# Cross attention of eight sequences: x in three buffers, first biases in step 4, h's high part behind the fourth head, and the mix's high part of the last step on VectorE

## The chip, the cores and the metric

The kernel runs on one core of a Trainium2 chip. The metric is the device time of one execution in microseconds (us). TensorE multiplies, VectorE, ScalarE and GpSimd (POOL) work element by element, SyncE (SP) issues most transfers.

## The reference

For eight sequences, x of 256 rows by 256 and a context of 256 rows by 192, with 16 heads of 64:

```python
h = _layernorm(x, gamma, beta)
Q = (h @ Wq).reshape(B, NQ, N_HEADS, HEAD_DIM)
K = (context @ Wk).reshape(B, NC, N_HEADS, HEAD_DIM)
V = (context @ Wv).reshape(B, NC, N_HEADS, HEAD_DIM)
attn = jnp.einsum('bihd,bjhd->bhij', Q, K)
attn = jax.nn.softmax(attn, axis=-1) * scale
vals = jnp.einsum('bhij,bjhd->bihd', attn, V).reshape(B, NQ, INNER)
out = vals @ Wo + bo
return x + out
```

## The kernel before

Every large product is made to near fp32 precision from two fp32r parts: an operand is rounded to its high part (ScalarE mostly), the remainder is its low part (VectorE or GpSimd), and TensorE sums high x high, high x low and low x high in PSUM.

The work is cut into 32 steps, four to a sequence; a step handles two pairs of heads, that is four heads. A program for each engine walks the steps -1 to 33 in the same order, and semaphores tie them together. In step u TensorE makes the scores of u (`scores`), mixes V with the probabilities of step u - 1 (`mix`), projects keys and queries of u + 1 (`keys`, `queries`), adds step u - 1's share of the output to `o_ps` (`output`), makes a tile of V two steps ahead or so (`values`) and turns the scaled probabilities of u (`turn`, L989). ScalarE takes the exponentials (L475), the high part of the mix (L502) and of keys and queries (L485), and copies half of the turned probabilities. VectorE takes the maxima (L674), the inverses of the sums (L681), the low part of the mix (L739) and of keys and queries (L699), scales the fourth head (L689) and copies the other half of the turned probabilities (L779). GpSimd scales the first three heads (L383).

Between these stand the jobs of a sequence, placed by `of_seq(u, offset)`: x and its context are loaded five steps before the sequence's first (`LOAD`), VectorE's statistics of x stand in that step too (`STATS`, L600), GpSimd's reciprocal deviation (L328) and norm (L336) one step later with TensorE's turn of the context, TensorE's turn of the normed x one more (`TURN_X`), h split into high part (VectorE, L760) and low part (GpSimd, L365) two steps ahead (`SPLIT_H`: steps 2, 6, ..., 26), and then GpSimd adds the output's bias to x (L352), which VectorE adds to the finished sum (L724) for the store. Sequences 0 and 1 have places of their own: statistics of 1 at the end of step 0, deviation and norm of 1 first in GpSimd's step 1, bias 0 at the end of GpSimd's step 2 and bias 1 at the end of step 4.

x has two buffers. SyncE's load of x of sequence 2 overwrites that of sequence 0, so it waits in step 3 for sequence 0's norm and bias (L286). The 25 pieces of the weights are loaded at the start and split during steps -1 to 4: the high parts on ScalarE (L423), the low parts on VectorE (L593) for the pieces in `LO_VECTOR` and on GpSimd (L322) for those in `LO_POOL`. Pieces 8, 9 and 20, 21 are Wv. For V, GpSimd copies the context's parts from `c_t` to `c_val` (L347).

PSUM has three pairs of banks in a ring, a bank for the mix and one for the output. In the last step with output through `output` (u = 31) the keys, queries and values of later steps are missing, so little stands between the mix and the output (L957); `last_output` (L973) ends the last sequence.

Of the kernel before, what the change touches and what calls it, by code (L numbers as in the profile page):

```python
# [6 lines left out]
def cross_attention_block(nc, x, ctx_in, w_q, w_k, w_v, w_o, b_o, gamma, beta, out):  # L7
# [10 lines left out]
    P = 128  # L18
# [15 lines left out]
    LOOP_STEPS, LOOPS = 2 * PER_SEQ, 3  # L34
# [27 lines left out]
    LO_VECTOR = (0, 4, 5, 8, 9, 13, 20, 21)  # L62
    LO_POOL = (1, 2, 3, 6, 7, 10, 11, 12, 14, 15, 16, 17, 18, 19, 22, 23)
    WARM = 6
    SHIFT = 16
    V_HALF = GROUP * P // 2

    with ExitStack() as ctx:
# [37 lines left out]
        x_in = sb("x_in", [P, 2, RT, D])  # L106
# [37 lines left out]
        x_banks = ring[2]  # L144
# [15 lines left out]
        x_loaded = [sem("x_loaded0"), sem("x_loaded1")]  # L160
# [53 lines left out]
        def walk(engine, step, first):  # L214

            for u in range(-1, first):
                step(u, lambda n: 0)
            with engine.Fori(0, LOOPS) as turn:  # L220
                for u in range(first, first + LOOP_STEPS):
                    step(u, lambda n: turn * n)
            for u in range(first + LOOP_STEPS * LOOPS, LAST):
                step(u, lambda n: 0)

# [16 lines left out]
        def _(sp):  # L242
            def number(n):
                return n if isinstance(n, int) else sp.snap(n)

# [20 lines left out]
            def load_x(b, sequence):  # L266
                sp.dma_start(x_in[:, b % 2, :, :], x_v[sequence]).then_inc(x_loaded[b % 2], 16)

            def load_c(b, sequence):
                sp.dma_start(c_in[:, b % 2, :, :], c_v[sequence]).then_inc(c_loaded[b % 2], 16)  # L270

            load_x(0, 0)
            for n in range(0, 10):
                load_weight(n)
            load_x(1, 1)
            load_c(1, 1)
# [3 lines left out]
            def step(u, turns):  # L280
                b = of_seq(u, LOAD, 2)
                if b is not None:
                    sequence, used = number(b + turns(2)), number(b - 1 + turns(2))

                    sp.wait_ge(x_norm_ready, used)
                    sp.wait_ge(x_bias_ready, used)  # L286
                    load_x(b, sequence)
                    sp.wait_ge(c_turned, used)
                    load_c(b, sequence)
                b = of_seq(u, PUT)  # L290
                if u == LAST - 1:

                    sp.wait_ge(y_ready, SEQS)
                    sp.dma_start(y_v[SEQS - 1, :, 0, :], y_sb[:, b % 2, 0, :])\
                        .then_inc(y_free[b % 2], 16)
                elif b is not None:
                    sequence, added = number(b + turns(2)), number(b + 1 + turns(2))
                    sp.wait_ge(y_ready, added)
                    sp.dma_start(y_v[sequence], y_sb[:, b % 2, :, :]).then_inc(y_free[b % 2], 16)

            walk(sp, step, 3)
# [5 lines left out]
        def _(pool):  # L307
# [23 lines left out]
            def norm(b):  # L331
# [3 lines left out]
                for r in range(RT):  # L335
                    last = nc.gpsimd.tensor_scalar(x_norm[:, r, :], x_in[:, b % 2, r, :],  # L336
# [4 lines left out]
            def context_for_values(b):  # L341

                if b >= 2:
# [6 lines left out]
            def bias(b):  # L350
                for r in range(RT):
                    last = nc.gpsimd.tensor_tensor(x_bias[:, b % 2, r, :], x_in[:, b % 2, r, :],  # L352
# [6 lines left out]
            pool.dma_start(bo_b[:, :], b_o.partition_broadcast(P)).then_inc(bo_in, 16)  # L359
            context_for_values(0)  # L360
# [8 lines left out]
            def step(u, turns):  # L369
# [3 lines left out]
                if b is not None:  # L373
                    deviation(b)
                    norm(b)
# [21 lines left out]
                b = of_seq(u, SPLIT_H, 1)  # L397
                if u == 2:
                    weight_lo(22)

                    pool.wait_ge(bo_in, 16)
                    bias(0)

                b = 1 if u == PER_SEQ else b if u > PER_SEQ else None
                if b is not None:
                    if b >= 2:

                        pool.wait_ge(y_ready, b - 1)

                    pool.wait_ge(x_norm_ready, b + 1)  # L410
                    bias(b)

            for u in range(-1, LAST):
                step(u, lambda n: 0)

        @block.scalar
        def _(act):
# [42 lines left out]
            def step(u):  # L460
# [39 lines left out]
                elif 1 <= u < STEPS:  # L500
# [85 lines left out]
        def _(dve):  # L586
# [10 lines left out]
            def rows_statistics(b, r):  # L597
                k = b % 2
                dve.wait_ge(x_loaded[k], 16 * (b // 2 + 1))
# [20 lines left out]
            def norm(b):  # L620
                dve.wait_ge(rstd_ready, b + 1)
                for r in range(RT):
                    last = nc.vector.tensor_scalar(x_norm[:, r, :], x_in[:, b % 2, r, :],
                                                   mean_var[:, r, 0:1], rstd[:, r:r + 1],
                                                   ALU.subtract, ALU.mult)
                last.then_inc(x_norm_ready, 1)
# [27 lines left out]
            def step(u):  # L654
# [73 lines left out]
                if u == 0:  # L728
                    weight_lo(8)
                    weight_lo(9)  # L730
                if u == STEPS:
# [5 lines left out]
                elif 1 <= u < STEPS:  # L737
# [16 lines left out]
                if u < 2:  # L754
                    last_head()
# [17 lines left out]
                if 0 <= u < STEPS:  # L773
# [8 lines left out]
                    if u == 0:  # L782
                        statistics(1)
# [330 lines left out]
```

## Time and profile before

| | us |
|---|---|
| median of 3 runs | 339.98 |
| lowest, highest run | 339.65, 396.95 |
| the profiled execution's own time | 339.38 |
| its span, first to last instruction | 337.3 |

The page counts the busy time of each engine inside the span; the time outside it, 2.1 us, is start and end of the program. Matmuls overlap, so TensorE's busy share says that it was supplied, not that it ran at its peak. "PEclk" is the granted clock in tenths of the full speed. In a list of instructions, a number in brackets is the idle time of the engine before the instruction, and what ended it.

### The profile page before, as it was taken

Reading aid. Unit: us, or ns where it says so; the run is one execution under the profiler, and the core shown is the slowest. Engines: PE = TensorE matmul, PEld = TensorE weight load, DVE = VectorE, ACT = ScalarE, POOL = GpSimd, SP = SyncE. Lnnn points to the kernel's source line nnn. Section 1 sums busy time; section 2 is a strip of 40 time slices with the busy share of each in tenths; the row PEclk is TensorE's granted clock in tenths of the full one; section 3 lists DMA queues with packets and bytes.
Section 4 is the critical chain, followed back from the end, with each engine's and each line's share of the span. In section 5 each row is a group of like instructions: output and inputs, shape, how many; then the busy total and the mean of one; then the engine's idle time right before and its main releaser. Section 6 shows DMA issues by size and latency. Waiting matters only on the chain.

```text
span 337.3 us, 9748 instructions
## 1 busy us (share of the span) xinstructions
PE 322.7 (96%) x3773; PEld 283.2 (84%) x3773; DVE 258.4 (77%) x585; ACT 254.7 (76%) x799; POOL 161.3 (48%) x294
## 2 busy tenths in 40 slices
PE   5999997999999999999999999999999999999986
PEld 4868777888889988888998888899888889988864
DVE  4898855787887788787877878877887878668764
ACT  4898883888778877787677887778777876777872
POOL 4688954463563364631563435633646315333330
PEclk9999997999999999999999999999999999999999
DMA  6860001020000200002000200002000010001000
GB/s 182 258 186 2 1 26 32 2 82 7 2 3 2 87 0 3 2 2 87 1 3 2 81 10 2 0 3 88 2 2 0 2 34 2 2 0 34 2 3 31
DMA packets 10764, 10.70 MB, mean 32 GB/s; under 512 B 960, under 2 KB 10176, under 8 KB 10720
## 3 DMA queue, kind: packets, MB, share of 16 engines
q1 hardware_dynamic: 10192, 9.64, 9.3%
q8 instruction: 30, 0.49, 0.6%
q10 hardware_dynamic: 416, 0.33, 0.3%
q0 software_dynamic: 112, 0.13, 0.2%
q14 instruction: 14, 0.11, 0.1%
HBM read 8.00 MB, written 2.10 MB: 30 GB/s over the span
## 4 chain that ended last, share of the span: by engine, by line
PE 78%; ACT 9%; DVE 6%; POOL 4%; issue 1%; DMA 1%; DVEq 0%; SPq 0%; POOLq 0%; ACTq 0%
PE mix_ps L866 15%; PE ring_ps L837 12%; PE ring_ps L932 11%; PE o_ps L957 10%; PE ring_ps L890 9%; PE ring_ps L989 8%; PE ring_ps L1023 6%; ACT prob L475 4%; DVE prob L689 2%; PE ring_ps L1030 2%; ACT qk_hi L485 2%; PE ring_ps L910 1%; PE o_ps L798 1%; POOL prob L383 1%; POOL wo_lo L322 1%
## 5 line engine op out<-in xcount | busy, mean ns | idle before, releaser
L383 POOL TENSOR_SCALAR prob<-prob,inv 128x256 f32<-128x256 f32 x192 | 90.3, 488 | 121.7 <-DVE inv L681 121.7
L475 ACT ACTIVATE prob<-ring_ps,neg_max 128x256 f32<-128x256 f32 x256 | 118.3, 474 | 21.7 <-DVE neg_max L674 21.7
L674 DVE TENSOR_REDUCE neg_max<-ring_ps 128x2 f32<-128x512 f32 x128 | 81.3, 677 | 1.0 <-PE ring_ps L837 0.8
L866 PE MATMUL mix_ps<-prob_t,v_sb 128*64 128x256 f32 x504 | 61.5, 385 | 0.5 <-DVE prob_t L779 0.5
L779 DVE COPY prob_t<-ring_ps 128x512 f32<-128x512 f32 x64 | 41.9, 687 | 21.6 <-PE ring_ps L989 20.3
L699 DVE TENSOR_TENSOR qk_lo<-ring_ps,qk_hi 128x512 fp32r<-128x512 f32 x64 | 44.1, 689 | 15.6 <-ACT qk_hi L485 15.6
L475 ACT ACTIVATION_READ_ACCUMULATOR prob<-ring_ps,neg_max 128x1 f32 x256 | 52.8, 206 | 0.0
L485 ACT ACTIVATE qk_hi<-ring_ps 128x512 fp32r<-128x512 f32 x64 | 38.7, 605 | 14.1 <-PE ring_ps L932 14.1
L866 PEld LDWEIGHTS mix_ps<-prob_t,v_sb 128*64 128x64 f32 x504 | 33.4, 136 | 18.3 <-issue 0.6
L989 PE MATMUL ring_ps<-ident,prob 64*128 64x64 f32 x1024 | 38.6, 223 | 1.8 <-DVE prob L689 1.1
L837 PE MATMUL ring_ps<-qk_hi 64*128 64x256 f32 x256 | 39.9, 301 | 0.3 <-DVE qk_lo L699 0.3
L957 PE MATMUL o_ps<-wo_hi,mix_hi 128*128 128x256 f32 x124 | 35.2, 284 | 4.3 <-DVE mix_lo L739 4.0
L989 PEld LDWEIGHTS ring_ps<-ident,prob 64*128 64x128 f32 x1024 | 36.2, 138 | 3.3 <-issue 1.7
L546 ACT ACTIVATE v_sb<-ring_ps 128x256 f32<-128x256 f32 x58 | 19.1, 381 | 25.9 <-PE ring_ps L1030 25.9
L560 ACT ACTIVATE prob_t<-ring_ps 128x512 f32<-128x512 f32 x64 | 35.8, 605 | 3.5 <-PE ring_ps L989 3.5
L837 PE MATMUL ring_ps<-qk_hi,qk_lo 64*128 64x256 f32 x256 | 36.8, 277 | 0.0
L837 PE MATMUL ring_ps<-qk_lo,qk_hi 64*128 64x256 f32 x256 | 36.8, 277 | 0.0
L890 PEld LDWEIGHTS ring_ps<-c_t,w_hi 128*128 128x128 f32 x192 | 26.5, 188 | 11.7 <-issue 11.5
L890 PE MATMUL ring_ps<-c_t,w_hi 128*128 128x256 f32 x192 | 35.5, 294 | 0.0
L957 PE MATMUL o_ps<-wo_lo,mix_hi 128*128 128x256 f32 x124 | 34.9, 281 | 0.0
L957 PE MATMUL o_ps<-wo_hi,mix_lo 128*128 128x256 f32 x124 | 34.8, 281 | 0.0
L681 DVE RECIPROCAL inv<-sums 128x2 f32<-128x2 f32 x128 | 20.9, 163 | 16.7 <-ACT prob L475 11.1
(116 smaller groups left out, 697.0 us busy)
## 6 DMA issues: line engine op xcount, KB each, us to landing
x_in<-in_x_dram SPq DMA_DIRECT2D x8, 256.0 KB, 2.9
out_dram<-y_sb SPq DMA_DIRECT2D x7, 256.0 KB, 2.2
c_in<-in_ctx_dram SPq DMA_DIRECT2D x7, 192.0 KB, 2.8
w_raw<-in_L_xattn_Wq_dram SPq DMA_DIRECT2D x8, 128.0 KB, 3.4
w_raw<-in_L_xattn_Wo_dram SPq DMA_DIRECT2D x4, 256.0 KB, 6.3
w_raw<-in_L_xattn_Wk_dram SPq DMA_DIRECT2D x4, 128.0 KB, 3.8
w_raw<-in_L_xattn_Wk_dram SPq DMA_DIRECT2D x8, 64.0 KB, 3.5
w_raw<-in_L_xattn_Wv_dram SPq DMA_DIRECT2D x2, 256.0 KB, 5.1
```

Of the source, the lines that this page charges most:

```text
L383: last = nc.gpsimd.tensor_scalar(prob[:, e, r, :], prob[:, e, r, :], inv[:, e, r:r + 1], SCALE, ALU.mult, ALU.mult)
L475: last = nc.scalar.activation(prob[:, e, r, :], score_bank(u, e)[:, r * ROWS:(r + 1) * ROWS], ACT.Exp, bias=neg_max[:, e, r:r + 1], accum_ ...
L485: nc.scalar.activation(qk_hi[:, a, :, 0:ROWS], qk_banks(u + 1)[a][:, :].rearrange("p (a b) -> p a b", b=ROWS), ACT.Copy)\
L674: nc.vector.tensor_reduce(neg_max[:, e, :], score_bank(u, e)[:, :].rearrange("p (r j) -> p r j", r=RT), AX, ALU.max, negate=True).then_inc ...
L699: nc.vector.tensor_tensor(qk_lo[:, a, :, 0:ROWS], qk_banks(u + 1)[a][:, :] .rearrange("p (a b) -> p a b", b=ROWS), qk_hi[:, a, :, 0:ROWS]. ...
L779: nc.vector.tensor_copy(turned_half(e), score_bank(u, e)[:, :] .rearrange("p (k i) -> p k i", i=HALF))\
L837: last = nc.tensor.matmul(score_bank(u, 2 * a + h)[:, r * ROWS:(r + 1) * ROWS], q[own, a, 1, r * P:(r + 1) * P], key[own, a, 0, 0:ROWS], s ...
L866: last = nc.tensor.matmul(ps[h * HALF:(h + 1) * HALF, first:first + ROWS], v_sb[:, w // RT % 2, j, p * P + h * HALF:p * P + (h + 1) * HALF ...
L890: nc.tensor.matmul(ps[:, 0:ROWS], w[:, i, cols], c_t[:, b % 2, k, :], start=not shared and w is w_hi and i == K0 and k == 0, stop=w is pas ...
L932: last = nc.tensor.matmul(ps[:, ROWS:2 * ROWS], w[:, Q0 + d, cols], h[:, b % 2, d, :], start=n == 0 and d == 0, stop=n == 2 and d == DT - ...
L957: last = nc.tensor.matmul(o_ps[:, r * D:(r + 1) * D], m[:, a, r * P:(r + 1) * P], wt[:, o, cols], start=s == 0 and a == 0 and n == 0 and r ...
L989: last = nc.tensor.transpose(score_bank(u, 2 * a + half)[:, k * HALF:(k + 1) * HALF], prob[own, 2 * a + h, r, j * P:(j + 1) * P], ident[ow ...
```

## The change

- x has three buffers, each with its semaphore. SyncE's loads of x wait for the norm and the bias of three sequences before; that of sequence 2 waits for nothing. The load of the bias vector `bo` moves from GpSimd's queue to SyncE's, behind the weights. SyncE's loop is written out.
- GpSimd's biases 0 and 1 both stand at the end of step 4.
- In steps from 2 on, VectorE makes h's high part behind the fourth head (behind both low parts of the keys and `deviation_base`). In step 2 its pieces 20 and 21 come ahead, right behind the first low part of the keys; `variance` of a measured sequence stands where it stood.
- Piece 8 is split on GpSimd before step 0 in place of VectorE in step 0. The values of sequence 0 read `c_t`; its copy to `c_val` is gone.
- The statistics of x 1 are spread over VectorE's step 0, and its norm goes from GpSimd to VectorE's step 1, one half on each side of the first low part of the keys.
- Around step 0 the ring's pairs of banks are named so that step 1's second pair of scores waits for the first pair's turned probabilities only.
- In step 31 VectorE makes the mix's high part (a copy) as well as its low part, with the third inverse between them; TensorE does the eight products of the high part first, then the four of the low part. The last output has its high products first too.

```diff
-    LO_VECTOR = (0, 4, 5, 8, 9, 13, 20, 21)
-    LO_POOL = (1, 2, 3, 6, 7, 10, 11, 12, 14, 15, 16, 17, 18, 19, 22, 23)
+    LO_VECTOR = (0, 4, 5, 9, 13, 20, 21)
+    LO_POOL = (1, 2, 3, 6, 7, 8, 10, 11, 12, 14, 15, 16, 17, 18, 19, 22, 23)
+    X_BUFS = 3
-        x_in = sb("x_in", [P, 2, RT, D])
+        x_in = sb("x_in", [P, X_BUFS, RT, D])
         def qk_banks(u):
-            return ring[u % 3]
+            return ring[u % 3 if u else 2]
         def score_bank(u, e):
-            return ring[(u - (e // 2 if u else 1 - e // 2)) % 3][e % 2]
+            return ring[(u - e // 2) % 3][e % 2]
-        x_banks = ring[2]
+        x_banks = ring[0]
...
             for n in range(10, len(PIECES)):
                 load_weight(n)
+            sp.dma_start(bo_b[:, :], b_o.partition_broadcast(P)).then_inc(bo_in, 16)
-            def step(u, turns):
+            def step(u):
                 b = of_seq(u, LOAD, 2)
                 if b is not None:
-                    sp.wait_ge(x_norm_ready, used)
-                    sp.wait_ge(x_bias_ready, used)
-                    load_x(b, sequence)
-                    sp.wait_ge(c_turned, used)
-                    load_c(b, sequence)
+                    if b >= X_BUFS:
+                        sp.wait_ge(x_norm_ready, b - X_BUFS + 1)
+                        sp.wait_ge(x_bias_ready, b - X_BUFS + 1)
+                    load_x(b)
+                    sp.wait_ge(c_turned, b - 1)
+                    load_c(b)
...
             def context_for_values(b):
-                if b >= 2:
+                if b >= 3:
                     pool.wait_ge(v_made, PER_SEQ * (b - 1))
...
             for n in (1, 2, 3, 6, 7):
                 weight_lo(n)
-            pool.dma_start(bo_b[:, :], b_o.partition_broadcast(P)).then_inc(bo_in, 16)
-            context_for_values(0)
+            weight_lo(8)
...
                 if b is not None:
                     deviation(b)
-                    norm(b)
+                    if b >= 2:
+                        norm(b)
...
                 if u == 2:
                     weight_lo(22)
-                    pool.wait_ge(bo_in, 16)
-                    bias(0)
-                b = 1 if u == PER_SEQ else b if u > PER_SEQ else None
-                if b is not None:
-                    if b >= 2:
-                        pool.wait_ge(y_ready, b - 1)
-                    pool.wait_ge(x_norm_ready, b + 1)
-                    bias(b)
+                for b in (0, 1) if u == PER_SEQ else (of_seq(u, SPLIT_H, 2),):
+                    if b is not None:
+                        if b == 0:
+                            pool.wait_ge(bo_in, 16)
+                        if b >= 2:
+                            pool.wait_ge(y_ready, b - 1)
+                        pool.wait_ge(x_norm_ready, b + 1)
+                        bias(b)
...
         @block.scalar
-                elif 1 <= u < STEPS:
+                elif 1 <= u < STEPS - 1:
                     act.wait_ge(mixed, u)
...
         @block.vector
                 if u == 0:
-                    weight_lo(8)
                     weight_lo(9)
+                    rows_statistics(1, 0)
...
-                elif 1 <= u < STEPS:
+                elif u == STEPS - 1:
+                    dve.wait_ge(mixed, u)
+                    nc.vector.tensor_copy(mix_hi[:, :, :].rearrange("p a b -> p (a b)"),
+                                          mix_ps[:, :]).then_inc(mix_hi_ready, 1)
+                    inverse(2)
+                if 1 <= u < STEPS:
                     dve.wait_ge(mix_hi_ready, u)
...
-                inverse(2)
+                if u != STEPS - 1:
+                    inverse(2)
...
+                if u == 1:
+                    dve.wait_ge(x_turned, 1)
+                    norm(1, (0,))
                 keys_lo(0)
+                if u == 0:
+                    rows_statistics(1, 1)
+                if u == 1:
+                    norm(1, (1,))
+                if u == 2:
+                    weight_lo(20)
+                    weight_lo(21)
                 if measured is not None:
                     variance(measured)
                 if u == -1:
                     weight_lo(5)
                 if u < 2:
                     last_head()
+                keys_lo(1)
+                if u == 0:
+                    variance(1)
+                if measured is not None:
+                    deviation_base(measured)
+                if u >= 2:
+                    last_head()
                 b = of_seq(u, SPLIT_H, 1)
                 if b is not None:
                     for d in range(DT):
                         dve.wait_ge(h_full_ready, DT * b + d)
                         nc.vector.tensor_copy(h_hi[:, b % 2, d, :], h_full[:, d, :])\
                             .then_inc(h_hi_ready, 1)
-                if u == 2:
-                    weight_lo(20)
-                    weight_lo(21)
-                keys_lo(1)
-                if measured is not None:
-                    deviation_base(measured)
-                if u >= 2:
-                    last_head()
...
                     if u == 0:
-                        statistics(1)
+                        deviation_base(1)
                         weight_lo(13)
...
             def scores(u):
-                            pe.wait_ge(prob_t_ready[h], BATCH * (u - 1) + (2 if u == 1 else 1))
+                            pe.wait_ge(prob_t_ready[h], BATCH * (u - 1) + 1)
...
             def output(w):
+                if w == STEPS - 2:
+                    pe.wait_ge(mix_hi_ready, w + 1)
+                    for m, weights in ((mix_hi, (wo_hi, wo_lo)), (mix_lo, (wo_hi,))):
+                        if m is mix_lo:
+                            pe.wait_ge(mix_lo_ready, w + 1)
...
             def last_output():
                 for a in range(BATCH):
-                    pe.wait_ge(mix_lo_ready, STEPS + a)
+                    pe.wait_ge(mix_hi_ready, STEPS + a)
                     for r in range(RT):
...
+                    pe.wait_ge(mix_lo_ready, STEPS + a)
+                    for r in range(RT):
...
             def values(n):
-                pe.wait_ge(c_val_ready, b + 1)
+                tiles = c_val if b else c_t
+                if b:
+                    pe.wait_ge(c_val_ready, b)
```

## Rows read from the trace of the kernel before

**Rows 1.** The page: busy time by engine with share; granted clock by slice.
```profile
PE 322.7 (96%) x3773; PEld 283.2 (84%) x3773; DVE 258.4 (77%) x585; ACT 254.7 (76%) x799; POOL 161.3 (48%) x294
PEclk9999997999999999999999999999999999999999
```

**Rows 2.** TensorE's waits over the span: us in total, times, longest.
```profile
PE o_ps L957 <- DVE mix_lo L739: 4.0, 2, 2.6
PE ring_ps L989 <- DVE prob L689: 1.1, 6, 0.2
```

**Rows 3.** Stretches: length; busy PE, PEld, DVE, ACT, POOL; granted clock; DMA.
```profile
12.56:20.72 8.16, 7.50 (x82) 6.11 (x84) 7.63 (x17) 8.08 (x27) 7.38 (x14) 1.00 0.83 263
...
43.76:57.72 13.96, 11.40 (x124) 10.15 (x120) 7.50 (x22) 7.99 (x26) 8.58 (x12) 0.88 0.12 34
...
77.68:87.56 9.88, 9.70 (x124) 8.51 (x120) 8.38 (x18) 7.46 (x24) 5.70 (x10) 1.00 0.00 1
87.56:97.09 9.53, 9.53 (x123) 8.45 (x121) 7.63 (x22) 6.82 (x24) 4.46 (x8) 1.00 0.01 2
```

**Rows 4.** Timeline of step 3: start, duration, then idle time and releaser last.
```profile
47.05 1.44 POOL L352 TENSOR_TENSOR x_bias<-x_in,bo_b 128x256 f32<-128x256 f32 x2
...
48.72 0.39 SPq L267 DMA_DIRECT2D x_in<-in_x_dram  x1
...
51.44 0.43 DVE L600 BATCH_NORM_STATS2 bn<-x_in 128x6 f32<-128x256 f32 x1 [3.67 <-DMA x_in<-in_x_dram]
...
52.60 0.55 PE L957 MATMUL o_ps<-wo_hi,mix_hi 128*128 128x256 f32 x1 [2.56 <-DVE mix_lo L739]
```

**Rows 5.** One stretch behind that wait, same columns.
```profile
53.00:54.00 1.00, 1.00 (x6) 1.00 (x6) 1.00 (x5) 0.00 (x0) 0.56 (x2) 0.50 0.00 0
```

**Rows 6.** Timeline of GpSimd: its first heads in step 9.
```profile
110.26 1.85 POOL L383 TENSOR_SCALAR prob<-prob,inv 128x256 f32<-128x256 f32 x4 [2.30 <-DVE inv L681]
```

**Rows 7.** Timeline of steps 6 and 7: h, fourth head, turned probabilities.
```profile
84.02 0.49 DVE L760 CAST h_hi<-h_full 128x256 fp32r<-128x256 f32 x2
84.59 1.44 POOL L365 TENSOR_TENSOR h_lo<-h_full,h_hi 128x256 fp32r<-128x256 f32 x2 [0.47 <-DVE h_hi L760]
85.58 1.33 DVE L689 TENSOR_SCALAR prob<-prob,inv 128x256 f32<-128x256 f32 x2
...
95.49 0.62 DVE L689 TENSOR_SCALAR prob<-prob,inv 128x256 f32<-128x256 f32 x2
96.92 1.29 DVE L779 COPY prob_t<-ring_ps 128x512 f32<-128x512 f32 x2 [0.81 <-PE ring_ps L989]
```

**Rows 8.** Timelines of GpSimd, TensorE and VectorE, steps -1 to 2.
```profile
13.71 0.60 POOL L359 DMA_DIRECT2D bo_b<-in_L_xattn_bo_dram  x1
14.32 1.08 POOL L347 CAST c_val<-c_t 128x256 fp32r<-128x256 f32 x3
...
17.88 0.73 PE L1011 MATMUL mix_ps<-wv_lo,c_val 128*128 128x512 f32 x2 [0.36 <-DVE wv_lo L593]
...
25.26 2.44 POOL L336 TENSOR_SCALAR x_norm<-x_in,mean_var,rstd 128x256 f32<-128x256 f32 x2 [0.19 <-POOL rstd L328]
...
30.55 0.71 PE L989 MATMUL ring_ps<-ident,prob 64*128 64x64 f32 x16 [0.27 <-POOL prob L383]
...
39.12 1.82 DVE L593 TENSOR_TENSOR wv_lo<-w_raw,wv_hi 128x512 fp32r<-128x512 f32 x2
...
41.00 0.74 PE L1011 MATMUL mix_ps<-wv_lo,c_val 128*128 128x512 f32 x2 [0.49 <-DVE wv_lo L593]
```

**Rows 9.** Timeline of the last steps: the mix's parts, the output, the last sums.
```profile
326.03 0.60 ACT L502 ACTIVATE mix_hi<-mix_ps 128x512 fp32r<-128x512 f32 x1
...
326.66 0.69 DVE L739 TENSOR_TENSOR mix_lo<-mix_ps,mix_hi 128x512 fp32r<-128x512 f32 x1 [0.33 <-ACT mix_hi L502]
...
327.41 0.38 PE L957 MATMUL o_ps<-wo_hi,mix_hi 128*128 128x256 f32 x1 [1.42 <-DVE mix_lo L739]
...
334.28 0.76 DVE L668 TENSOR_TENSOR y_sb<-ring_ps,y_sb 128x256 f32<-128x256 f32 x2 [0.78 <-PE ring_ps L973]
```

More of the change, by code:

```diff
@@ L33, in cross_attention_block @@
     STEPS = SEQS * PER_SEQ
-    LOOP_STEPS, LOOPS = 2 * PER_SEQ, 3
     LAST = STEPS + 2
@@ L159, in cross_attention_block @@
         w_in = [sem(f"w_in{i}") for i in range(len(PIECES))]
-        x_loaded = [sem("x_loaded0"), sem("x_loaded1")]
+        x_loaded = [sem(f"x_loaded{k}") for k in range(X_BUFS)]
         c_loaded = [sem("c_loaded0"), sem("c_loaded1")]
@@ L212, in of_seq @@
             return b if rest == 0 and first <= b < SEQS else None
[L214 to L224, printed above, removed]
         def before(n, pieces):
@@ L296, in step @@
                 elif b is not None:
[L297 to L301, printed above, removed]
+                    sp.wait_ge(y_ready, b + 1)
+                    sp.dma_start(y_v[b], y_sb[:, b % 2, :, :]).then_inc(y_free[b % 2], 16)
+            for u in range(-1, LAST):
+                step(u)
             sp.wait_ge(y_free[0], 16 * (SEQS // 2 + 1))
@@ L367, in hidden_lo, with step @@
                                             ALU.subtract).then_inc(h_lo_ready, 1)
-            def step(u, turns):
+            def step(u):
                 if u == 1:
@@ L618, in statistics, with norm @@
                 deviation_base(b)
-            def norm(b):
+            def norm(b, rows=range(RT)):
                 dve.wait_ge(rstd_ready, b + 1)
-                for r in range(RT):
-                    last = nc.vector.tensor_scalar(x_norm[:, r, :], x_in[:, b % 2, r, :],
+                for r in rows:
+                    last = nc.vector.tensor_scalar(x_norm[:, r, :], x_in[:, b, r, :],
                                                    mean_var[:, r, 0:1], rstd[:, r:r + 1],
                                                    ALU.subtract, ALU.mult)
-                last.then_inc(x_norm_ready, 1)
+                if r == RT - 1:
+                    last.then_inc(x_norm_ready, 1)
             def context_lo(b, ps):
@@ L949, in output @@
                     pe.wait_ge(y_ready, b)
+                if w == STEPS - 2:
[3 more added lines that the diff above has]
+                            pe.wait_ge(mix_lo_ready, w + 1)
+                        for a in range(BATCH):
+                            o, cols = divmod(BATCH * s + a, GROUP)
+                            cols = slice(cols * D, (cols + 1) * D)
+                            for r in range(RT):
+                                for wt in weights:
+                                    last = nc.tensor.matmul(
+                                        o_ps[:, r * D:(r + 1) * D], m[:, a, r * P:(r + 1) * P],
+                                        wt[:, o, cols], start=False, stop=False,
+                                        skip_group_check=True)
+                    last.then_inc(o_added, 1)
+                    return
                 pe.wait_ge(mix_lo_ready, w + 1)
@@ L966, in last_output @@
                 for a in range(BATCH):
[L967 removed]
                     o, cols = divmod(PAIRS - BATCH + a, GROUP)
                     cols = slice(cols * D, (cols + 1) * D)
+                    pe.wait_ge(mix_hi_ready, STEPS + a)
                     for r in range(RT):
[L971 to L976 removed]
+                        for n, wt in enumerate((wo_hi, wo_lo)):
+                            nc.tensor.matmul((ring[2][1], ring[1][0])[r][:, 0:D],
+                                             mix_hi[:, a, r * P:(r + 1) * P], wt[:, o, cols],
+                                             start=a == 0 and n == 0, stop=False,
+                                             skip_group_check=True)
+                    pe.wait_ge(mix_lo_ready, STEPS + a)
+                    for r in range(RT):
+                        last = nc.tensor.matmul((ring[2][1], ring[1][0])[r][:, 0:D],
+                                                mix_lo[:, a, r * P:(r + 1) * P], wo_hi[:, o, cols],
+                                                start=False, stop=a == BATCH - 1,
+                                                skip_group_check=True)
                         if a == BATCH - 1:
@@ L1010, in values @@
                             low_ready(pe, FOR_V[g])
-                        last = nc.tensor.matmul((mix_ps, o_ps, mix_ps)[n][:, :], c_val[:, b % 2, k, rows],
+                        last = nc.tensor.matmul((mix_ps, o_ps, mix_ps)[n][:, :], tiles[:, b % 2, k, rows],
                                                 w[:, i, first:first + PIECE],
@@ L1022, in values @@
                             low_ready(pe, FOR_V[g])
-                        nc.tensor.matmul(ps[:, 0:V_HALF], c_val[:, b % 2, k, rows],
+                        nc.tensor.matmul(ps[:, 0:V_HALF], tiles[:, b % 2, k, rows],
                                          w[:, i, first + a * V_HALF:first + (a + 1) * V_HALF],
@@ L1026, in values @@
                 pe.wait_ge(c_rest_ready, b + 1)
-                high = (c_rest[:, b % 2, rows], c_val[HALF:P, b % 2, 1, rows])
+                high = (c_rest[:, b % 2, rows], tiles[HALF:P, b % 2, 1, rows])
                 for a, ps in enumerate(qk_banks(n)):
```

34 lines of the change are left out of this document (12 added, 22 removed).

## The prediction

> **What bounds the kernel now.** I read the page's engine table and its forty slices first. TensorE is busy 96% of 337.3 us, no other engine over 77%, and the granted clock stands at its full level except in one slice [rows 1]. So only stretches in which TensorE waits or runs at the low clock can give time back; work saved elsewhere counts only if it ends such a stretch. The list of TensorE's waits names two kinds that this change touches: the output products waiting for the mix's low part, 4.0 us in two places, and the transposes of probabilities waiting for the fourth head, six times [rows 2].
>
> Next I cut the span at the starts of the scores of one step to those of the next. Step 7, from 87.56 us, has nothing special: 9.53 us with TensorE never idle. Step 3, from 43.76, does the same TensorE work in 13.96 us; step 6, from 77.68, again the same work, takes 9.88 us, with 0.18 us of idle in it [rows 3]. Those excesses, 4.43 us and 0.35 us, are the two large terms below. Steps 0 to 2 and the last step I read in the timeline.
>
> **Step 3: x in three buffers, first bias later.** The chain is: GpSimd adds the first bias at 47.05 us for 1.44 us; only then may SyncE issue x of sequence 2, at 48.72; VectorE sits 3.67 us until it lands and starts its statistics at 51.44; the low part of the mix stands behind them, and TensorE starts the output at 52.60 after 2.56 us of idle [rows 4]. The idle is followed by a granted clock of 0.50, which is 1.2 GHz [rows 5]; that is why the step lost more than its idle. With a third buffer x of sequence 2 has a place of its own, and SyncE issues it right behind the weights with no wait at all. c of sequence 2 behind it waits only for the turn of c 0, long done; the result of sequence 0 is next in that queue and is not wanted before step 5. When this stall goes, what is late next in step 3? The same queue of VectorE as in step 7, where its statistics stand in the same place and TensorE never waits. The low part of Wo for that step is made on GpSimd ahead of where the bias was, so it isn't moved back; the heads on GpSimd come 1.44 us earlier. So step 3 becomes a step 7: minus 4.43 us (bounds 2.56, if the low clock stays for another reason, and 4.43).
>
> What this costs elsewhere: biases 0 and 1 both stand at the end of GpSimd's step 4, 2 x 1.44 = 2.88 us instead of 1.44. In the step that answers to it four steps on (no bias there) GpSimd idles 2.30 us before its first heads [rows 6]; so they start 2.88 - 2.30 = 0.6 us late. These heads are in place long before TensorE turns them at the end of a step of 10 us. Zero; with that cover gone it would be 0.6 us once. The load of the bias vector moves from GpSimd's queue to the end of SyncE's, where only step 4 needs it. Later x loads wait for an older bias than before: zero.
>
> **The high part of h behind the fourth head (steps 2, 6, ..., 26).** Now VectorE makes h's high part at 84.02 (0.49 us for two), GpSimd at once makes the low part at 84.59 (1.44 us) and then a bias, and the fourth head's two scalings, which begin at 85.58, take 1.33 us; one step on, with GpSimd idle, the same two take 0.62 us [rows 7]. The 0.71 us reach TensorE as the 0.18 us of idle before the second half of its turn, and with what stands behind that, as 0.35 us of the step [rows 3]. With h behind the fourth head GpSimd waits until the scalings are over. The two h copies, 0.49 us, then fall in the 0.81 us that VectorE waits before its copy of turned probabilities [rows 7], so nothing is pushed. GpSimd's low part moves about 2.5 us, to the end of the step; the queries that use it are in the next step, after scores and mix. Six such steps stand between 77 us and 284 us (the six waits of [rows 2]): 6 x 0.35 = 2.1 us, and the step 2 case is counted with the start. Bounds 0 (the collision just takes another form) and 2.1 us, since a step like step 7 has no idle left to give.
>
> The Trainium skill, SBUF — State Buffer, section "Who interferes with whom", says that GpSimd and a VectorE scaling or cast in its two-port mode exclude each other for a whole instruction, and that a copy out of PSUM isn't among these. The trace agrees in size, 1.33 us against 0.62 us. By the rule the moved h copies, with GpSimd idle, cost their 0.49 us; if they met GpSimd's work they would double to about 1 us, which is past the cover of 0.81 us.
>
> **The start, steps 0 to 2.** Step 0: VectorE drops one of two splits of Wv, so TensorE's low Wv products, which start at 17.88, can start 0.5 us earlier; GpSimd takes that split (128x512, two inputs: as much as the two 128x256 of h, 1.44 us [rows 7]) and loses the bias DMA, 0.60, and the first copy of c, 1.08 us [rows 8]: even. VectorE's statistics of x 1, two of 0.43 us [rows 4] and small ones, go between other work of step 0; they push the fourth head and the low part of the keys a little, so of the 0.5 us about 0.25 are left at the step's end. Reading c_t in place of the copy changes no size. The bank names swapped around step 0 remove a wait that TensorE, busy turning c, doesn't feel now.
> Step 1: GpSimd's norm of x 1 takes 2.44 us, and its heads behind it hold TensorE's turn of the probabilities, its second half to 30.55 [rows 8]. On VectorE the same norm is two scalings, 0.62 us free and 1.33 us against GpSimd [rows 7]. That frees GpSimd and puts VectorE's fourth head in its place as the last: 0.4 to 0.9 us gained, I take 0.65 with the 0.25 of step 0 included, as VectorE is now the tight one.
> Step 2: VectorE's two splits of Wv at 39.12 take 1.82 us beside GpSimd's work, and TensorE waits 0.49 us for the second [rows 8]. Moved ahead of the two h copies (0.49 us [rows 7]) they end at least that much earlier, so the wait goes: 0.5 us, bounds 0 and 0.9 us. Together the start gives 1.15 us, bounds 0.2 and 2.
>
> **The last two steps.** Now ScalarE makes the high part at 326.03 (0.60 us), VectorE the low part at 326.66 (0.69), and TensorE, idle 1.42 us, starts at 327.41 [rows 9]. VectorE can't begin the high part before two inverses, at about 326.25; a copy of 512 from PSUM to SBUF costs it about 0.65 us (its copies of turned probabilities, 1.29 us for two [rows 7]), so TensorE starts its eight high products at about 327.0 and finds the low part made at about 327.8, ready when they are through: 0.4 us. ScalarE is 0.5 us ahead with the third and fourth head's probabilities, so the turn behind isn't late. I take 0.45 us. The last output with high products first: its last sums run on VectorE one after the other, 0.76 us for both [rows 9], and the first can't start much earlier; 0.1 us. Together 0.55 us, bounds 0 and 1.
>
> **Sum.** 4.43 + 2.1 + 1.15 + 0.55 = 8.2 us. The profiled execution itself took 339.38 us, 2.1 us more than its span and 0.6 us less than the shown median of 339.98: 339.4 - 8.2 = 331.2 us. No engine takes a new load on the path, and as TensorE has no idle in a step like step 7, nothing gained early is given back later.
>
> **Rivals.**
> Start or end don't pay. ScalarE is busy 8.08 of step 0's 8.16 us [rows 3]; if it or VectorE's new norm ends last, the 1.15 + 0.55 us shrink to about 0.2: 332.7 us. Against it: in step 1 it is GpSimd that TensorE waits for.
> The h move only shifts the collision, to the copy behind or the next step's heads: 2.1 us stay, 333.3 us. For it: GpSimd still has the same work beside VectorE; against it: the 0.81 us of cover.
> Step 3 gives only its idle: another wait of half a microsecond there, or a low clock all the same, leaves 1.9 us: 333.1 us.
> TensorE bound and the change without effect: if the 96% were true work, nothing moves, 339.4 us. Against it: 13.96 us against 9.53 for the same instructions.
> Slower: the third x buffer shifts every tensor behind it in SBUF by 2 KB a partition, the probabilities that TensorE turns among them. A step has 32 such pairs of transposes in about 1 us; were they slower by over a quarter (8.2 us over 32 steps is 0.26 us a step), the gain would be gone, and at double time it would be 339.4 - 8.2 + 32 = 363 us. No row shows a dependence on place, so this is the least likely.
>
> **How the numbers follow.** Forecast 0.60; start and end without pay 0.14; h 0.09; step 3 in part 0.08; without effect 0.06; slower 0.03. The likeliest gives 331.2. Low: start and end at their upper bounds give 0.85 + 0.45 = 1.3 us more, 329.9; for places where TensorE waits less than these rows show I go 0.9 us further, to 329.0. High: the cases at 333.3, with 333.6. A time faster by 2% is under 333.2 us (about what a measurement of this kernel can tell from no change). The forecast, the start case, and some half of the two cases at that edge lie below it, less a little for two small losses together: 0.76; within 2%: 0.21; slower: 0.03.
>
> **What would show it.** Right: step 3 at about 9.5 us with no low clock after the start; x of sequence 2 landed by about 25 us; steps 6, 10, ... at 9.5 us with the fourth head's scalings at 0.62 us for two; no wait on GpSimd's heads in step 1; the last output's wait near 1.0 us. Wrong: a wait of VectorE for x, copies of turned probabilities that start later than 0.81 us behind the fourth head, transposes that take longer everywhere, or a new low-clock stretch.

## The result and the profile after

| us | before | after |
|---|---|---|
| median | 339.81 (4 runs) | 331.37 (4 runs, 331.17 to 331.65) |
| profiled execution | 339.38 | 331.32 |
| its span | 337.3 | 329.3 |

One of the four runs before took 396.95 us, a slow run, and the ratio leaves it out; the other three lie between 339.49 and 339.98. The ratio is 0.9755, with a 95% interval of 0.9736 to 0.9774. On another chip the kernel after took 331.21 us (5 runs, 331.04 to 331.4), ratio 0.9764 [0.9741, 0.9788]. The forecast was 331.2.

The page of the kernel after, engine table and granted clock, to be laid beside [rows 1]:

```profile
PE 319.2 (97%) x3773; PEld 281.7 (86%) x3773; DVE 253.8 (77%) x587; ACT 253.2 (77%) x798; POOL 155.5 (47%) x289
PEclk9999999999999999999999999999999999999999
```

The slice at the low clock is gone. TensorE's waits in the kernel after:

```profile
PE ring_ps L1015 <- DVE prob L676: 1.0, 1, 1.0
PE o_ps L965 <- DVE mix_hi L727: 1.0, 1, 1.0
PE mix_ps L870 <- DVE prob_t L783: 0.5, 1, 0.5
```

The six waits of 0.2 us for the fourth head and the one of 2.6 us [rows 2] are gone. One wait for the fourth head, of 1.0 us, is new; it stands in step 1 and was not foreseen. The stretches from one step's scores to the next, with the columns of [rows 3]; they are steps 0, 1, 2, 3 and 6, 7:

```profile
12.50:20.13 7.63, 7.30 (x83) 6.20 (x84) 7.31 (x20) 7.56 (x26) 5.82 (x10) 1.00 0.96 272
20.13:31.83 11.70, 10.48 (x121) 8.59 (x118) 10.62 (x25) 10.23 (x32) 8.23 (x13) 1.00 0.32 98
31.83:43.14 11.31, 11.03 (x123) 9.56 (x123) 7.98 (x19) 9.78 (x31) 6.70 (x11) 1.00 0.01 1
43.14:52.72 9.58, 9.58 (x123) 8.51 (x120) 7.90 (x22) 7.98 (x26) 6.87 (x13) 1.00 0.00 0
72.68:82.19 9.51, 9.51 (x124) 8.43 (x120) 7.34 (x18) 7.07 (x24) 3.27 (x7) 1.00 0.01 3
82.19:91.70 9.51, 9.51 (x124) 8.43 (x120) 7.82 (x22) 7.08 (x24) 6.75 (x12) 1.00 0.01 2
```

Steps 3, 6 and 7 are now alike, 9.58, 9.51 and 9.51 us. From the starts of the scores in the two timelines (steps 1, 2, 3, 4 and 31: 20.72, 31.77, 43.76, 57.72 and 322.45 us before; 20.13, 31.83, 43.14, 52.73 and 315.03 after) and the two spans, each term can be read by itself:

| place | gain, measured in the two traces | forecast |
|---|---|---|
| up to the end of step 1 | -0.06 us (up to the end of step 0: +0.59; step 1: -0.65) | 0.65 |
| step 2 | 0.68 | 0.5 |
| step 3 | 4.37 | 4.43 |
| steps 4 to 30, six of them with h | 2.43 | 2.1 |
| from step 31 on | 0.58 | 0.55 |
| sum | 8.0 | 8.2 |

### The profile page after: what moved, and what is told of

Its sections match the earlier page's. It is cut to its first block, busy times and chain, and to the rows that moved or that the text cites. A ratio compares the mean times of both kernels' runs of the same rounds, so it can differ in the third digit from the quotient of the medians.

```text
span 329.3 us, 9691 instructions
## 1 busy us (share of the span) xinstructions
PE 319.2 (97%) x3773; PEld 281.7 (86%) x3773; DVE 253.8 (77%) x587; ACT 253.2 (77%) x798; POOL 155.5 (47%) x289
## 4 chain that ended last, share of the span: by engine, by line
PE 88%; ACT 5%; DVE 3%; POOL 2%; issue 1%; DVEq 0%; POOLq 0%; ACTq 0%
PE mix_ps L870 16%; PE ring_ps L841 13%; PE o_ps L978 12%; PE ring_ps L936 12%; PE ring_ps L894 10%; PE ring_ps L1015 9%; PE ring_ps L1052 8%; PE ring_ps L1059 3%; ACT prob L461 3%; PE ring_ps L914 1%; PE o_ps L802 1%; PE mix_ps L815 1%; PE mix_ps L807 1%; DVE prob_t L783 1%; DVE qk_lo L686 1%
## 5 line engine op out<-in xcount | busy, mean ns | idle before, releaser
L370 POOL TENSOR_SCALAR prob<-prob,inv 128x256 f32<-128x256 f32 x192 | 89.0, 480 | 106.1 <-DVE inv L668 105.9
L783 DVE COPY prob_t<-ring_ps 128x512 f32<-128x512 f32 x64 | 41.2, 686 | 21.0 <-PE ring_ps L1015 21.0
L1015 PE MATMUL ring_ps<-ident,prob 64*128 64x64 f32 x1024 | 37.5, 223 | 1.0 <-DVE prob L676 1.0
L978 PE MATMUL o_ps<-wo_hi,mix_hi 128*128 128x256 f32 x120 | 33.3, 278 | 0.5 <-POOL wo_lo L309 0.3
L978 PE MATMUL o_ps<-wo_lo,mix_hi 128*128 128x256 f32 x120 | 33.3, 277 | 0.0
L978 PE MATMUL o_ps<-wo_hi,mix_lo 128*128 128x256 f32 x120 | 33.2, 276 | 0.0
```

What stands on the lines that cost most here:

```text
L370: last = nc.gpsimd.tensor_scalar(prob[:, e, r, :], prob[:, e, r, :], inv[:, e, r:r + 1], SCALE, ALU.mult, ALU.mult)
L783: nc.vector.tensor_copy(turned_half(e), score_bank(u, e)[:, :] .rearrange("p (k i) -> p k i", i=HALF))\
L978: last = nc.tensor.matmul(o_ps[:, r * D:(r + 1) * D], m[:, a, r * P:(r + 1) * P], wt[:, o, cols], start=s == 0 and a == 0 and n == 0 and r ...
L1015: last = nc.tensor.transpose(score_bank(u, 2 * a + half)[:, k * HALF:(k + 1) * HALF], prob[own, 2 * a + h, r, j * P:(j + 1) * P], ident[ow ...
```

## The experiments

**The third buffer alone.** On the kernel before: x in three buffers, SyncE's load of x 2 free, bias 0 moved.

```diff
-                    sp.wait_ge(x_norm_ready, used)
-                    sp.wait_ge(x_bias_ready, used)
+                    if b >= 3:
+                        sp.wait_ge(x_norm_ready, b - 2)
+                        sp.wait_ge(x_bias_ready, b - 2)
...
                     weight_lo(22)
+                if u == PER_SEQ:
                     pool.wait_ge(bo_in, 16)
+                    pool.wait_ge(x_norm_ready, 2)
                     bias(0)
```

> The kernel before with only the third buffer for x, SyncE's load of x 2 without a wait, and bias 0 moved to the end of step 4. Theory A (the load of x 2 behind the first bias is the whole excess of step 3, idle and low clock): step 3 falls from 13.96 to about 9.55 us and the time by 4.4, to 335.5 us. Rival B (the idle goes but the low clock or another wait of the step stays): a fall of 2.6 us, to 337.3 us. Rival C (the gains of the other parts hang on this one or the other way round): less than 2 us or more than 6.

335.22 us, ratio 0.9881 [0.9854, 0.9907] to the kernel before on that chip (339.36), which is 4.1 us. Its step 3 runs from 43.49 to 53.24 us, 9.75. Theory A holds; half of the whole gain is this one load. The profiled execution was the slowest of the four (335.94 us), and its steps 3, 7, 8 and 27 to 30 each took 0.13 to 0.18 us longer than in the traces of the kernels before or after, at full clock. What slows them is not known.

**The wait, not the buffer.** The kernel after, in which SyncE's load of x 2 waits all the same: for bias 0, put back to the end of step 2, and in a second kernel only for GpSimd's low part of piece 22, which ends earlier.

```diff
                 if b is not None:
+                    if b == 2:
+                        sp.wait_ge(x_bias_ready, 1)
...
                     weight_lo(22)
-
-                for b in (0, 1) if u == PER_SEQ else (of_seq(u, SPLIT_H, 2),):
+                    pool.wait_ge(bo_in, 16)
+                    bias(0)
+
+                for b in (1,) if u == PER_SEQ else (of_seq(u, SPLIT_H, 2),):
```

> The kernel after, with bias 0 back at the end of step 2 and SyncE's load of x 2 waiting for it although its buffer is free. Theory A (the wait, not the buffer, is the cost): TensorE idles about 2.6 us in step 3, the clock then falls to half, the step takes about 14 us, 335.8 us in all. Rival B (the low clock before had another cause, such as the order of the start): idle of 2.6 us but full clock, 334.0 us.

```diff
                 if b is not None:
+                    if b == 2:
+                        sp.wait_ge(w_lo_pool_ready, before(23, LO_POOL))
```

> The kernel after, with SyncE's load of x 2 waiting for GpSimd's low part of piece 22, 1.4 us before where bias 0 would end. Theory A (part of the price is the clock that falls behind a long wait): TensorE idles about 1.3 to 1.6 us; if the clock holds, the time is 332.8 us, if it falls as it did behind 2.6 us, 334.5 us. This run tells whether the half wait already pays the clock.

One execution each: 335.82 us with the full wait, 332.88 with the half. TensorE's wait in the first, then the granted clock (third value from the end) behind it:

```profile
51.75 0.36 PE L982 MATMUL o_ps<-wo_hi,mix_hi 128*128 128x256 f32 x1 [2.35 <-DVE mix_lo L736]
...
53.00:54.00 1.00, 1.00 (x7) 1.00 (x6) 0.96 (x5) 0.00 (x0) 0.51 (x1) 0.50 0.00 0
```

And in the second:

```profile
50.49 0.36 PE L980 MATMUL o_ps<-wo_hi,mix_hi 128*128 128x256 f32 x1 [1.08 <-DVE mix_lo L734]
...
51.00:52.00 1.00, 1.00 (x11) 1.00 (x10) 1.00 (x6) 0.00 (x0) 0.44 (x1) 1.00 0.00 0
```

Behind 2.35 us of idle the clock stood at 0.50, its lower level of 1.2 GHz; behind 1.08 us it stayed full. The step took 13.77 us (43.18 to 56.95) with the full wait and 11.02 (43.18 to 54.20) with the half. With its free buffer in place the kernel pays the old price as soon as the load waits again, which is theory A; one execution of each kernel says so. The half wait also costs more than its idle: the first output product stands 7.31 us into the step in place of 6.05 in the kernel after (49.19 - 43.14), 1.26 us later where the trace counts 1.08.

**h's high part, undone.** The kernel after with the two copies back ahead of the keys' second low part.

```diff
+                b = of_seq(u, SPLIT_H, 1)
+                if b is not None:
+                    for d in range(DT):
+                        dve.wait_ge(h_full_ready, DT * b + d)
+                        nc.vector.tensor_copy(h_hi[:, b % 2, d, :], h_full[:, d, :])\
+                            .then_inc(h_hi_ready, 1)
                 keys_lo(1)
...
                 if u >= 2:
                     last_head()
-                b = of_seq(u, SPLIT_H, 1)
-                if b is not None:
...
```

> The kernel after with one part undone: VectorE makes h's high part again ahead of the second low part of the keys, in steps 2, 6, ..., 26. Theory A: each of the six steps from 6 to 26 goes back to about 9.9 us, the time rises by 2.1 to 2.4, to 333.6 us, and the fourth head's two scalings take 1.33 us there. Rival B (the move brought nothing, the gain came from the smaller queue of GpSimd): 331.4 us.

333.77 us, ratio 0.9838 [0.9811, 0.9864]. Step 6 in its timelines of VectorE, GpSimd and TensorE:

```profile
79.38 1.44 POOL L351 TENSOR_TENSOR h_lo<-h_full,h_hi 128x256 fp32r<-128x256 f32 x2 [0.48 <-DVE h_hi L765]
80.37 1.33 DVE L676 TENSOR_SCALAR prob<-prob,inv 128x256 f32<-128x256 f32 x2
...
81.86 0.71 PE L1015 MATMUL ring_ps<-ident,prob 64*128 64x64 f32 x16 [0.18 <-DVE prob L676]
```

The pattern of [rows 7] is back, 1.33 us and 0.18 us of idle, and with it 2.4 to 2.5 us: theory A.

**Is it VectorE's order or GpSimd's neighbour?** The same kernel as h_back, but GpSimd holds h's low part, and so the bias behind it, until the fourth head is scaled.

```diff
                 pool.wait_ge(h_hi_ready, DT * b)
+                pool.wait_ge(scaled_vector, PER_SEQ * b + SPLIT_H + 1)
```

> The same as h_back, VectorE's order as before, but GpSimd holds h's low part until the fourth head is scaled. Theory A (the cost is GpSimd's two-input subtraction running beside VectorE's scalings, not VectorE's order): the scalings take 0.62 us, the steps 9.5 us, 331.4 us as the kernel after. Rival B (the cost is that h's two copies stand ahead of the keys' second low part and the fourth head): 333.6 us as h_back.

331.31 us (331.28 to 331.32), on the same chip as the 333.77. In its step 6:

```profile
78.81 0.48 DVE L766 CAST h_hi<-h_full 128x256 fp32r<-128x256 f32 x2
79.25 0.69 DVE L687 TENSOR_TENSOR qk_lo<-ring_ps,qk_hi 128x512 fp32r<-128x512 f32 x1
80.17 0.17 DVE L669 RECIPROCAL inv<-sums 128x2 f32<-128x2 f32 x1 [0.22 <-ACT prob L462]
80.36 0.62 DVE L677 TENSOR_SCALAR prob<-prob,inv 128x256 f32<-128x256 f32 x2
```

VectorE's order is that of the kernel before, its scalings take 0.62 us, and all of the gain is there: theory A again. So the move of h was worth its 2.4 us only because it kept GpSimd's work, the subtraction and the start of the bias behind it, off VectorE's scalings; a wait on GpSimd does the same.

**The norm of x 1 back on GpSimd.**

```diff
                     deviation(b)
-                    if b >= 2:
-                        norm(b)
+                    norm(b)
...
-                if u == 1:
-                    dve.wait_ge(x_turned, 1)
-                    norm(1, (0,))
                 keys_lo(0)
-                if u == 1:
-                    norm(1, (1,))
```

> The kernel after with the norm of x 1 back on GpSimd in step 1. Theory A (the move paid nothing: TensorE's turn began at 30.60 us with it and at 30.55 before): 331.4 us, within 0.4, with TensorE now waiting for GpSimd's heads. Rival B (the prediction's term for step 1, hidden by something else in the kernel after): 332.0 us.

330.96 us (330.68 to 330.98), 0.35 less than the 331.31 of h_back_hold on the same chip, whose step 1 is that of the kernel after (11.73 us against 11.70). GpSimd and TensorE in step 1:

```profile
27.45 2.80 POOL L369 TENSOR_SCALAR prob<-prob,inv 128x256 f32<-128x256 f32 x6
...
30.30 0.71 PE L1008 MATMUL ring_ps<-ident,prob 64*128 64x64 f32 x16 [0.26 <-POOL prob L369]
```

Within the 0.4 us of theory A, but on the side of a small loss: moved as it was, the norm cost 0.35 us. That is not all of step 1's loss. Steps 0 and 1 of this kernel, laid beside the 8.16 and 11.05 us of the kernel before:

```profile
12.52:20.12 7.60, 7.30 (x82) 6.16 (x82) 7.27 (x20) 7.53 (x26) 5.79 (x10) 1.00 0.86 254
20.12:31.53 11.41, 10.56 (x122) 8.57 (x118) 9.71 (x23) 10.21 (x32) 10.49 (x15) 1.00 0.35 105
```

With GpSimd's norm where it was, step 1 still takes 0.36 us more than before.

**GpSimd's subtractions of step 1 behind the fourth head.** The kernel after, one wait more:

```diff
+                if u == 1:
+                    pool.wait_ge(scaled_vector, 2)
                 for n in {0: (10, 11, 12), 1: (15, 16, 17, 18)}.get(u, ()):
                     weight_lo(n)
```

> The kernel after, with GpSimd in step 1 holding the low parts of the weights' pieces 15 to 18 until the fourth head is scaled. Theory A (the norm's move was worth its price, but the freed GpSimd started these subtractions at 28.78 us, on the fourth head's scalings, 1.39 us in place of 0.62): the scalings take 0.62 us, TensorE's turn begins its second half at about 29.9 in place of 30.60, the time falls by 0.7, to 330.7 us. Rival B (ScalarE's or GpSimd's later work sets the end of step 2 anyway): 331.4 us.

330.13 us, ratio 0.9728 [0.9705, 0.9751]. Step 1 in the kernel after, VectorE, GpSimd and TensorE:

```profile
28.54 0.42 DVE L609 TENSOR_SCALAR x_norm<-x_in,mean_var,rstd 128x256 f32<-128x256 f32 x1
28.78 1.52 POOL L309 TENSOR_TENSOR w_lo<-w_raw,w_hi 128x256 fp32r<-128x256 f32 x2
29.06 1.39 DVE L676 TENSOR_SCALAR prob<-prob,inv 128x256 f32<-128x256 f32 x2
30.60 0.71 PE L1015 MATMUL ring_ps<-ident,prob 64*128 64x64 f32 x16 [1.01 <-DVE prob L676]
```

and in this one:

```profile
28.83 0.61 DVE L678 TENSOR_SCALAR prob<-prob,inv 128x256 f32<-128x256 f32 x2
29.53 1.42 POOL L309 TENSOR_TENSOR w_lo<-w_raw,w_hi 128x256 fp32r<-128x256 f32 x2 [0.95 <-DVE prob L678]
...
29.59 0.71 PE L1017 MATMUL ring_ps<-ident,prob 64*128 64x64 f32 x16 [0.24 <-DVE prob L678]
```

The scalings fall from 1.39 to 0.61 us and TensorE's wait from 1.01 to 0.24, which is theory A. Because the two kernels had run on different chips, both ran again on one:

> The kernel after, unchanged, on the same chip as hold_again: 331.4 us.

> The same kernel as hold_w, beside the kernel after on the same chip. Theory A (GpSimd's subtractions on the fourth head of step 1 cost the kernel after about 1 us, as the first run showed): 330.3 us against 331.4. Rival B (part of the first run's 1.2 us was a difference between chips): 330.7 us or more.

331.21 us (331.04 to 331.4) and 330.37 us (330.12 to 330.51). So 0.84 us; the first comparison's 1.24 held some 0.4 us of difference between chips, and 330.37 lies between the two expectations, near the first. This kernel is faster than the one before and the one after, than the latter by 0.84 of 331.21 us, a quarter of a per cent. Its steps 0 and 1:

```profile
12.27:19.88 7.61, 7.29 (x83) 6.17 (x83) 7.28 (x20) 7.53 (x26) 5.80 (x10) 1.00 0.86 258
19.88:30.83 10.95, 10.52 (x122) 8.61 (x118) 9.85 (x25) 10.27 (x32) 8.09 (x13) 1.00 0.38 115
```

**The last step undone.**

```diff
-                elif 1 <= u < STEPS - 1:
+                elif 1 <= u < STEPS:
                     act.wait_ge(mixed, u)
...
-                elif u == STEPS - 1:
-                    dve.wait_ge(mixed, u)
-                    nc.vector.tensor_copy(mix_hi[:, :, :].rearrange("p a b -> p (a b)"),
-                                          mix_ps[:, :]).then_inc(mix_hi_ready, 1)
-                    inverse(2)
...
-                if u != STEPS - 1:
-                    inverse(2)
+                inverse(2)
...
-                if w == STEPS - 2:
+                if False:
```

> The kernel after with step 31 undone: ScalarE makes the mix's high part, TensorE does high and low products mixed; the last output stays as changed. Theory A (the two edits of the end gave 0.45 and 0.1 us): the wait for the mix's low part is 1.4 us in place of 0.98 + 0, and the time rises by 0.45, to 331.8 us. Rival B (the whole 0.6 us of the end came from the last output): 331.4 us.

331.78 us (331.61 to 331.85), against 331.37 and 331.21 for the kernel after on two other chips: 0.4 to 0.6. VectorE and TensorE in the kernel after:

```profile
318.83 0.67 DVE L727 CAST mix_hi<-mix_ps 128x512 fp32r<-128x512 f32 x1
...
319.55 0.38 PE L965 MATMUL o_ps<-wo_hi,mix_hi 128*128 128x256 f32 x1 [0.98 <-DVE mix_hi L727]
...
320.58 0.62 PE L965 MATMUL o_ps<-wo_hi,mix_lo 128*128 128x256 f32 x4
```

and in this one, whose step 31 stands at the same time to 0.01 us:

```profile
319.25 0.69 DVE L726 TENSOR_TENSOR mix_lo<-mix_ps,mix_hi 128x512 fp32r<-128x512 f32 x1 [0.34 <-ACT mix_hi L488]
...
319.99 0.39 PE L971 MATMUL o_ps<-wo_hi,mix_hi 128*128 128x256 f32 x1 [1.42 <-DVE mix_lo L726]
```

TensorE starts 0.44 us earlier with the change, and the low products at 320.58 follow the high ones without a wait. This is theory A; the last output alone is worth about 0.1 us.

**The place of the tensors.** The kernel before with a third buffer for x that nothing uses.

```diff
-        x_in = sb("x_in", [P, 2, RT, D])
+        x_in = sb("x_in", [P, 3, RT, D])
```

> The kernel before with x declared with three buffers and only two of them used, so that every tensor behind it stands 2 KB further on in each partition and nothing else changes. Theory A (the place of the tensors costs nothing): 339.8 us, steps as before. Rival B (the rival on the slower side: the turn of the probabilities depends on their place): a rise, up to 24 us more at double time.

338.88 us (10 runs) against 339.46 (15 runs) for the kernel before on that chip; the ratio is 0.9999 [0.9976, 1.0023]. The shift costs nothing that these runs can tell. The 24 us of the expectation is the rival's figure with the gain taken off; turns at double time would have added some 32 us here.

## Why the prediction was right, and which term was not

**Step 3** was right in mechanism and size, 4.37 us for 4.43. SyncE now issues x of sequence 2 right behind the weights:

```profile
19.45 0.47 SPq L264 DMA_DIRECT2D bo_b<-in_L_xattn_bo_dram  x1
19.96 0.44 SPq L251 DMA_DIRECT2D x_in<-in_x_dram  x1
```

and nothing is late next in that step. Bias 0 and 1 in one piece took 2.79 us at 63.49 and pushed GpSimd's heads of step 5, as expected, without a wait of TensorE. The lower bound of 2.56 us, idle without clock, also describes real executions; see the last section.

**h behind the fourth head** was right in mechanism, and a little too small: 2.43 us for 2.1. The term was read from 9.88 - 9.53; against the 9.51 us of step 6 in the kernel after it is 0.37 us a step, 2.2 us for six. The other 0.2 us are spread over the rest of steps 4 to 30, 0.01 or 0.02 us in many of them, and no run says why. The cover held: the fourth head and the h copies of step 6 in the kernel after,

```profile
80.59 0.61 DVE L676 TENSOR_SCALAR prob<-prob,inv 128x256 f32<-128x256 f32 x2
81.12 0.49 DVE L772 CAST h_hi<-h_full 128x256 fp32r<-128x256 f32 x2
82.02 1.29 DVE L783 COPY prob_t<-ring_ps 128x512 f32<-128x512 f32 x2 [0.41 <-PE ring_ps L1015]
```

leave 0.41 of the 0.81 us [rows 7]. The rule of the Trainium skill, SBUF — State Buffer, section "Who interferes with whom", that a GpSimd instruction and a two-port scaling of VectorE exclude each other, agrees with h_back_hold: GpSimd's wait alone, with VectorE's order kept, brought 1.33 back to 0.62 us. The runs show that the two engines' work must not meet; that the port is the reason is the rule's part.

**Step 1 was the term that failed.** The prediction took 0.65 us for "GpSimd's norm to VectorE", step 0's share included; the two steps gave -0.06. It priced the norm itself fairly, 0.59 and 0.42 us for its two halves, and saw that VectorE would be last. What it left out is what a freed GpSimd does next: it began its subtractions of weights at 28.78 us, in place of 30.46 before and of 30.21 in norm_back, and so set two of them on the very scalings that TensorE waits for. It was the collision that the prediction had described for step 6, made anew in step 1. The wait of hold_w removed it, and 0.84 us came back (after_again against hold_again). With that wait steps 0 and 1 take 18.56 us in place of 19.21, and the 0.65 us of the forecast are there.

Step 0 gave more than its 0.25 us: TensorE's low products of Wv start at 17.32 in place of 17.88 and nothing after them is late. The prediction had expected VectorE's fourth head to be pushed; it took 0.62 us in place of 0.85 and ended earlier. In the traces GpSimd's heads, which end before it now, took 3.19 us in place of 3.84; no run takes the edits of step 0 one by one.

Most of that gain doesn't reach the end of step 1 while the norm stands on GpSimd: steps 0 and 1 of norm_back take 19.01 us, 0.20 less than before. ScalarE, busy 7.56 of step 0's 7.63 us in the kernel after, makes the weights' high parts at the old times, and GpSimd's low part waits for them. From there to its heads GpSimd has no wait over 0.2 us:

```profile
22.08 0.74 POOL L322 TENSOR_TENSOR w_lo<-w_raw,w_hi 128x256 fp32r<-128x256 f32 x1 [0.63 <-ACT w_hi L423]
...
22.03 0.73 POOL L309 TENSOR_TENSOR w_lo<-w_raw,w_hi 128x256 fp32r<-128x256 f32 x1 [0.64 <-ACT w_hi L408]
```

The first line is from the kernel before, whose heads start at 27.68, the second from norm_back, whose heads start at 27.45. So the norm's move is worth 0.45 us (19.01 - 18.56) if GpSimd's subtractions wait, near the lower end of the 0.4 to 0.9 that the prediction gave it. Its sentence that nothing gained early is given back later was wrong for steps 0 and 1, and so was the one that no engine takes a new load on the path, since VectorE took the norm.

**Step 2 and the end** were as forecast: the second Wv split no longer stops TensorE (0.68 for 0.5 us), the last step 0.44 us for 0.4 to 0.45, the last output about 0.1. h's move has no share in step 2, which takes 11.29 us in h_back and 11.31 in the kernel after; the split's own move was not undone by itself.

**The sum** is closer than its terms. 8.0 us for 8.2 came out because the 0.71 us missing up to step 2 were met by 0.33 more from h and 0.18 more from step 2; that part is luck. The chance of 0.76 for a time under 333.2 us is also less than its own chances give (0.60 + 0.14 + half of 0.17 is 0.83).

**The rivals.** "Start or end don't pay" described steps 0 and 1 rightly, and both engines that it named, ScalarE and VectorE with its new norm, had a share; step 2 (0.68 us) and the end (0.58 us) did pay. The h move did not shift its collision in step 6. "Step 3 gives only its idle" did not come true in the profiled execution. "Slower by the place of the tensors" is answered by pad_x, "without effect" by the result.

## What to carry to other kernels

Read a long wait with the clock behind it: here a load that waited for a bias that no one needed yet cost half of all that was gained, and the fix is a buffer and a later bias. When VectorE's short scaling between SBUF tensors stands ahead of TensorE, look at what GpSimd runs at that moment, and again after each edit that makes GpSimd earlier. One wait that holds GpSimd's uncritical work behind the scaling was worth 0.8 us in one step and 2.4 us in six, without moving anything on VectorE.

## What the runs showed of the hardware

The clock did not fall in every execution of the kernel before. Of 15 on one chip, 11 had a mean granted clock of 0.994 or 0.995 and took 338.85 to 340.48 us; 4 had 0.999 or 1.000 and took 337.51 to 337.63. On two other chips it was 7 of 9 and 8 of 9 at the lower clock. So the 2.56 us of idle [rows 4] costs about 1.9 us more or nothing, as much as the profiled step 3 lost beyond its idle (4.43 - 2.56 = 1.87), and the gain of the change over an execution whose clock held is 337.6 - 331.2 = 6.4 us. In pad_x the clock held in 4 of 10 executions, and the groups are less clear: 337.74 to 338.80 us there, 338.80 to 339.80 in the others. No trace of an execution whose clock held was kept, so that its wait was as long is inferred from the times. The runs of any one kernel without that wait lay within 0.5 us on one chip, but for x_three with 0.9. Behind 1.08 us of idle the clock held in the one execution seen. This fits the Trainium skill, TensorE: Matmul & The Clock Gate, section "Part 1: The HAM clock gate", by which the activity window is free-running, so that the same kernel meets it at another phase each time; no run here shows the window itself.

Where the work of the two engines met, VectorE paid. Its two scalings, 0.62 us free, took 1.33 us beside GpSimd's subtractions and the bias behind them (h_back) and 1.39 us beside its subtractions of weights (after, step 1). GpSimd's own pairs took 1.44 and 1.51 us (h_back) and 1.52 us (after), against 1.43 (h_back_hold) and 1.42 (hold_w) when they were held.
